# Second attention of a two-layer network: a query projection is given a PSUM bank of the other pair

## The chip, the cores and the metric

The kernel runs on one core of a Trainium2 chip. The metric is the device time of one execution in microseconds (us), the median of several; less is better.

## The reference

The reference takes 32 sequences of 128 tokens with 128 features and applies two layers, each of an attention and a feed-forward part with conditioning, all in fp32. The change lies in the attention of the second layer. That attention has 16 heads of 8 features, a causal mask and a layer norm:

```python
Q = jax.nn.relu(x @ Wq + bq)
K = jax.nn.relu(x @ Wk + bk)
V = jax.nn.relu(x @ Wv + bv)
...
scores = jnp.einsum('bqhd,bkhd->bhqk', Qh, Kh) / np.sqrt(dh)
...
attn = jax.nn.softmax(scores, axis=-1)
...
out = jnp.einsum('bhqk,bkhd->bqhd', attn, Vh).reshape(B, T, U)
out = out + x
...
return gamma * normalized + beta
```

Keys and queries whose token sums to zero are masked. The result is then multiplied by a per-sequence matrix (a base matrix plus a product of rank 8) before the last feed-forward part.

## The kernel before

The kernel is one program in which each engine has its own list of instructions, written out by hand, and the engines meet by counting semaphores. The second attention runs from about 645 to 856 us. It works in 32 blocks, one for each sequence; block q has four units of four heads (units 4q to 4q+3). Eight chunks of four sequences share one projection each of queries and keys.

Block q computes, spread over the engines:

- TensorE (`pe_attend2`): the scores of sequence q (`pe_S5`, L2113, 16 small matmuls into banks PB0 to PB3), the transposes of two units of the block before (`pe_T5`, units 4q-4 and 4q-3, L2141), in some blocks transposes of tokens or of the norm's output (L2249, L2343), the values of sequence q+1 (`pe_v5`, L2207), the product of weights and values of sequence q-2 (`pe_PV5`, L2158), in some blocks a projection (query L1623, key L1635, token sum L1632) or a product beside it (factors L2282 and L2288, select L2356, add L2367 and L2370), the transposes of units 4q-2 and 4q-1, and last the transposes of the attention's output of sequence q-2 (`pe_oT`, L2171).
- VectorE (`dve_attend2`): the norm of sequence q-3 (`dve_norm5`, L2180 to L2187), mask and maximum of the four units of block q (`dve_max5`, L2122, 16 instructions), with the layer norm's gamma step between the second and the third unit in every fourth block (`dve_gamma5`, L2349), then the bias of the values of sequence q+1 (`dve_v5`, L2212), statistics (L2199, L2201), and the steps beside (token-sum mask of the keys L1647, masks L2259 to L2263, factors L2300 and others).
- ScalarE (`act_attend2`): exponentials (L2134), the copies of transposed units out of PSUM (`act_pt5`, L2147), the copy of the attention's output (`act_o5`, L2165), the relu of a query or key projection (L1629, L1641), right behind that copy, and the norm's scaling (L2336).
- GpSimd (`pool_attend2`): subtraction of the maximum (L2129), relu and mask of the values (`pool_v5`, L2220 and L2221), a residual add (L2194) and the norm's root (L2325 to L2330).

The PSUM banks PB4 to PB7 are two pairs. A plan (`plan5`) walks through the program in TensorE's order and gives each result the next bank of its pair; `passes5` also records which semaphore says that the bank has been read out. Before a result is written, TensorE waits until the result two places earlier in the same pair has been read:

```python
def passes5(key, first, sem, value):
    through5[key] = first, len(drained5[first])
    drained5[first].append((sem, value))
...
def pe_drained5(key):
    first, n = through5[key]
    if n >= 2:
        pe.wait_ge(*drained5[first][n - 2])
```

The pair of PB4 and PB5 holds transposed units, the product with the values, queries and keys. The pair of PB6 and PB7 holds values, turned outputs, tokens, gamma, select, add, factors and the token sum. There are seven query projections in the plan: chunk 1 in block 1, chunk 2 in block 4, and chunks 3 to 7 in blocks 8, 12, 16, 20 and 24. The first chunk's was done before the attention began. The factors of the per-sequence matrices come in blocks 2, 3 and 4.

VectorE's bias of the values of sequence q+1 writes one of two buffers, so it waits (`dve.wait_ge(s_vy, 2 * (q - 2) + 1)`) until GpSimd has read the values two sequences earlier. For sequence 2, in block 1, that is GpSimd's first values step, which needs the masks of chunk 0.

Of the kernel before, what the change touches and what calls it, by code (L numbers as in the profile page):

```python
# [58 lines left out]
def build(nc, xT_d, w_d, out_d):  # L59
# [4 lines left out]
    with ctx:  # L64
# [3 lines left out]
        def signal(name):  # L68
            return ctx.enter_context(nc.semaphore(name))
# [897 lines left out]
        s_qp, s_qt, s_qz, s_be = signal("q_mm"), signal("q_relu"), signal("spread_zero"), signal("beta")  # L967
# [1051 lines left out]
# [3 lines that stand above are left out]

        def plan_aside(what, c):
            if what == "query":
                passes5(("q", c), 4, s_qt, c + 1)
            if what == "key":
                passes5(("k", c), 4, s_kt, c + 1)
            if what == "keysum":
                passes5(("ks", c), 6, s_kx, c + 1)
            if what == "tokens":  # L2030
                passes5(("x", c), 6, s_xc, c + 1)
            if what == "b1":
                passes5("b1", 6, s_b1, 3)
            if what == "factors":
                passes5(("f", c), 6, s_facd, c + 1)
            if what == "gamma":
                passes5(("T", c), 6, s_fd, 3 * c + 1)
            if what == "select":
                passes5(("A", c), 6, s_fd, 3 * c + 2)
            if what == "add":  # L2040
                passes5(("B", c), 6, s_fd, 3 * c + 3)

        def plan_asides(q, kinds):
            for s in range(4 * q, 4 * q + 4):
                for what, c in aside(s):
                    if what in kinds:
                        plan_aside(what, c)
# [9 lines left out]
        def plan5():  # L2057
            passes5(("x", 0), 6, s_xc, 1)
            passes5(("v", 0), 6, s_vt, 1)
            for q in range(NB5):  # L2060
                plan_T5(4 * q - 4)
                plan_T5(4 * q - 3)
                plan_asides(q, TURNED)
                if q + 1 < NB5:
                    passes5(("v", q + 1), 6, s_vt, q + 2)
                if q >= 2:
                    passes5(("o", q - 2), 4, s_o5, q - 1)
                plan_asides(q, PROJECTED)
                plan_asides(q, MULTIPLIED)
                plan_T5(4 * q - 2)  # L2070
                plan_T5(4 * q - 1)
                if q >= 2:
                    passes5(("oT", q - 2), 6, s_nd, 4 * (q - 2) + 4)
            for u in range(U - 4, U):
                plan_T5(u)
                if u == U - 4:
                    passes5(("o", NB5 - 2), 4, s_o5, NB5 - 1)
                if u == U - 3:
                    plan_aside("gamma", 6)
            passes5(("oT", NB5 - 2), 6, s_nd, 4 * (NB5 - 2) + 4)  # L2080
            plan_aside("select", 6)
            passes5(("o", NB5 - 1), 4, s_o5, NB5)
            passes5(("oT", NB5 - 1), 6, s_nd, 4 * (NB5 - 1) + 4)
            plan_aside("add", 6)
            for what in FINISH.values():
                plan_aside(what, 7)
# [1158 lines left out]
```

## Time and profile before

| | us |
|---|---|
| median of 3 runs | 955.68 |
| lowest and highest | 955.13, 956.82 |
| the profiled execution, its own time | 954.23 |
| its span on the core | 952.9 |
| mean granted TensorE clock, share of full | 0.996 |

| engine | busy us | share of the span |
|---|---|---|
| PE (TensorE matmul) | 918.1 | 96% |
| PEld (TensorE weight load) | 734.3 | 77% |
| DVE (VectorE) | 789.0 | 83% |
| ACT (ScalarE) | 796.1 | 84% |
| POOL (GpSimd) | 548.5 | 58% |

All times in the rows are us from the start of the span. A matmul row gives its start and the time until its modelled end; the next matmul may start before that end, since matmuls are pipelined. So the pace of TensorE is read from the starts. A bracket at a row's end says how long the engine sat idle before it and which instruction ended that. SPq is the queue of DMA issues.

### The profile page before, as it was taken

What the parts mean: (1) busy time and instruction counts of PE and PEld (TensorE: products, weight loads), DVE (VectorE), ACT (ScalarE), POOL (GpSimd) and SP (SyncE); (2) the same over time, 40 slices, a digit from 0 to 9 for tenths busy, and PEclk for the clock granted to TensorE, in tenths of its full rate; (3) what the DMA queues carried; (4) which work ended last, traced back from release to release, by engine and by line L of the source; (5) the groups of instructions that cost most, each with busy time, mean ns of one, the idle gap of its engine ahead of it and who ended that gap; (6) DMA issues with size and microseconds to landing.
All of it is one profiled execution on the core that took longest, in us unless ns stands there. A gap on an engine that the chain in (4) does not pass through costs nothing.

```text
span 952.9 us, 25813 instructions
## 1 busy us (share of the span) xinstructions
PE 918.1 (96%) x8641; PEld 734.3 (77%) x8641; DVE 789.0 (83%) x3563; ACT 796.1 (84%) x2162; POOL 548.5 (58%) x670
## 2 busy tenths in 40 slices
PE   8999999999999999999999999999989999999887
PEld 8899989899998989973225888877877777775566
DVE  6766998989898989989997766758889889896985
ACT  7998989898988888867875989987788888886886
POOL 4444636465564646451796148757789898891041
PEclk9999999999999999999999999999999999999899
DMA  9100000000000000000236899911000000000002
GB/s 372 69 2 2 2 2 2 2 2 2 2 1 2 2 2 2 2 2 0 89 115 195 283 304 306 318 63 33 24 20 18 24 17 21 24 3 1 2 1 89
DMA packets 36226, 57.70 MB, mean 61 GB/s; under 512 B 3456, under 2 KB 27264, under 8 KB 35712
## 3 DMA queue, kind: packets, MB, share of 16 engines
q1 hardware_dynamic: 36096, 56.07, 17.6%
q8 instruction: 69, 1.13, 0.5%
q14 instruction: 61, 0.50, 0.2%
HBM read 40.85 MB, written 11.01 MB: 54 GB/s over the span
## 4 chain that ended last, share of the span: by engine, by line
PE 64%; DVE 17%; ACT 9%; POOL 4%; issue 4%; DMA 0%; SPq 0%; ACTq 0%; DVEq 0%; POOLq 0%
PE PB L270 6%; PE PB L271 5%; PE PB L272 5%; PE PB L437 5%; PE PB L2141 5%; PE PB L390 4%; PE PB L459 3%; PE PB L2113 3%; PE PB L2158 3%; DVE W L400 2%; ACT W L409 2%; PE PB L1423 2%; PE PB L1424 2%; PE PB L1425 2%; DVE HFXT L607 1%
## 5 line engine op out<-in xcount | busy, mean ns | idle before, releaser
L409 ACT ACTIVATE W<-W,small 128x128 f32<-128x128 f32 x384 | 149.0, 392 | 11.4 <-DVE small L400 10.6
L421 POOL TENSOR_TENSOR W<-W,small 128x512 f32<-128x512 f32 x96 | 100.7, 1054 | 100.2 <-DVE small L415 100.2
L270 PE MATMUL PB<-RR_s 128*128 128x256 f32 (+1 forms) x468 | 153.2, 327 | 3.4 <-DVE RR_s L471 1.4
L271 PE MATMUL PB<-RR_s 128*128 128x256 f32 (+1 forms) x468 | 140.0, 299 | 0.0
L272 PE MATMUL PB<-RR_s 128*128 128x256 f32 (+1 forms) x468 | 139.8, 299 | 0.0
L2129 POOL TENSOR_TENSOR AR_s<-AR_s,small 128x512 f32<-128x512 f32 x128 | 129.9, 1045 | 15.4 <-DVE small L2122 15.4
L2122 DVE CUSTOM_DVE_ANT_0 AR_s<-PB,W 128x128 f32<-128x128 f32 x512 | 111.2, 286 | 2.1 <-PE PB L2113 0.3
L270 PEld LDWEIGHTS PB<-RR_s 128*128 128x128 f32 x468 | 88.8, 190 | 19.0 <-issue 7.8
L1399 DVE TENSOR_TENSOR RR_s<-AR_s,RR_s 128x512 fp32r<-128x512 f32 (+1 forms) x96 | 65.7, 689 | 43.0 <-ACT RR_s L1392 39.1
L400 DVE CUSTOM_DVE_ANT_0 W<-PB,W 128x128 f32<-128x128 f32 x384 | 85.9, 282 | 13.5 <-PE PB L390 12.8
L349 DVE COPY AR_s<-PB 128x512 f32<-128x512 f32 x128 | 84.9, 684 | 13.6 <-PE PB L272 13.0
L271 PEld LDWEIGHTS PB<-RR_s 128*128 128x128 f32 x468 | 89.0, 190 | 3.5 <-issue 0.7
L272 PEld LDWEIGHTS PB<-RR_s 128*128 128x128 f32 x468 | 88.6, 189 | 3.0
L2134 ACT ACTIVATE AR_s<-AR_s 128x512 f32<-128x512 f32 x128 | 79.7, 625 | 10.6 <-POOL AR_s L2129 10.1
L2147 ACT ACTIVATE AR_s<-PB 128x512 f32<-128x512 f32 x128 | 72.5, 593 | 17.8 <-PE PB L2141 17.5
L443 ACT ACTIVATE HFXT<-PB 128x512 f32<-128x512 f32 x123 | 73.4, 597 | 16.7 <-PE PB L437 14.6
L2141 PEld LDWEIGHTS PB<-W,AR_s 128*128 128x128 f32 x512 | 56.5, 141 | 26.7 <-issue 12.2
L2141 PE MATMUL PB<-W,AR_s 128*128 128x128 f32 x512 | 70.9, 278 | 5.2 <-ACT AR_s L2165 2.7
L409 ACT ACTIVATION_READ_ACCUMULATOR W<-W,small 128x1 f32 x384 | 73.2, 191 | 0.0
L1457 POOL TENSOR_TENSOR HFXT<-HFXT,AR_s 128x128 f32 x68 | 41.3, 636 | 54.5 <-DVE AR_s L1447 54.4
L390 PE MATMUL PB<-AR_s 64*128 64x128 f32 x1024 | 65.8, 278 | 0.0
L1392 ACT ACTIVATE RR_s<-AR_s 128x512 fp32r<-128x512 f32 (+1 forms) x96 | 57.3, 597 | 8.5
(461 smaller groups left out, 2635.0 us busy)
## 6 DMA issues: line engine op xcount, KB each, us to landing
RR_s<-W1D SPq DMA_DIRECT2D x13, 512.0 KB, 4.3
RR_s<-W2D SPq DMA_DIRECT2D x13, 512.0 KB, 4.5
W<-in_w SPq DMA_DIRECT2D x1, 5895.5 KB, 24.9
RR_s<-XD SPq DMA_DIRECT2D x46, 128.0 KB, 3.0
XD<-RR_s SPq DMA_DIRECT2D x18, 256.0 KB, 3.6
HQ<-W1D SPq DMA_DIRECT2D x6, 512.0 KB, 4.3
HQ<-W2D SPq DMA_DIRECT2D x6, 512.0 KB, 4.8
HQ<-XD SPq DMA_DIRECT2D x22, 128.0 KB, 3.2
```

The costliest lines, as they stand in the source:

```text
L270: nc.tensor.matmul(out, lh, rh, start=True, stop=False)
L271: nc.tensor.matmul(out, ll, rh, start=False, stop=False)
L272: return nc.tensor.matmul(out, lh, rl, start=False, stop=True)
L349: nc.vector.tensor_copy(QK[v % 2][pr], bank("k", n)[:, :]).then_inc(s_qk, 1)
L390: mm = nc.tensor.matmul(score(u, h), qk[r, b * 128:b * 128 + 128], qk[r, 256 + b * 128:256 + b * 128 + 128], start=True, stop=True)
L400: nc.vector.tensor_tensor_reduce(SS[r][:, hl], score(u, h), w("mask"), -0.125, 3.0e38, ALU.add, ALU.min, mx[r][:, h:h + 1]).then_inc(s_max, 1)
L409: e = nc.scalar.activation(SS[r][:, hl], SS[r][:, hl], ACTF.Exp, bias=mx[r][:, h:h + 1], scale=-1.0, accum_out=rc[r][:, h:h + 1])
L421: nc.gpsimd.tensor_tensor(s3, s3, over(rc[r], 2, [128, 4, 128]), ALU.mult).then_inc(s_nrm, 1)
L2122: nc.vector.tensor_tensor_reduce(SS5[r][:, hl], score5(u, h), w("mask"), isq8, -3.0e38, ALU.add, ALU.max, mx5[r][:, h:h + 1]).then_inc(s_m ...
L2129: nc.gpsimd.tensor_tensor(s3, s3, over(mx5[r], 2, [128, 4, 128]), ALU.subtract).then_inc(s_sub, 1)
L2134: nc.scalar.activation(SS5[r], SS5[r], ACTF.Exp).then_inc(s_ex5, 1)
L2141: mm = nc.tensor.transpose(bank5(("p", u))[:, hl], SS5[u % 6][:, hl], ident)
```

## The change

The query projection of a chunk is planned in the pair PB6 and PB7 where it was planned in PB4 and PB5. One number of the plan changes:

```diff
         def plan_aside(what, c):
             if what == "query":
-                passes5(("q", c), 4, s_qt, c + 1)
+                passes5(("q", c), 6, s_qt, c + 1)
             if what == "key":
                 passes5(("k", c), 4, s_kt, c + 1)
             if what == "keysum":
```

No instruction is added, removed or moved on any engine. What changes is the bank of each result behind a query, and, since each result waits for the one two places earlier in its pair, what TensorE waits for around each of the seven queries. In the rows below `v5_bias` is the semaphore of VectorE's bias of the values (L2212), `pt5` that of ScalarE's copy of a transposed unit (L2147), `o5` that of the copy of the output (L2165), `q_relu` and `k_relu` those of the relus (L1629, L1641), `norm5` that of VectorE's norm (L2180 to L2187), and `finish_dve` here that of the gamma step (L2349).

The first place is TensorE in block 1, from the values of sequence 2 to the scores of block 2. Before:

```order
L2207 MATMUL PB7<-W,HFXT 128x128 [waits v5_bias]
L1623 MATMUL PB4<-HFXT,W 128x512 [waits pt5]
L1635 MATMUL PB5<-HFXT,W 128x512 [waits pt5]
L1632 MATMUL PB6<-HFXT,small 128x512 [waits v5_bias]
L2141 MATMUL PB4<-W,AR_s5 128x128 [waits exp5,q_relu]
L2141 MATMUL PB4<-W,AR_s5 128x128 x3
L2141 MATMUL PB5<-W,AR_s5 128x128 [waits exp5,k_relu]
L2141 MATMUL PB5<-W,AR_s5 128x128 x3
L2113 MATMUL PB0<-KR0,QS0 128x128 [waits max5]
```

With the change:

```order
L2207 MATMUL PB7<-W,HFXT 128x128 [waits v5_bias]
L1623 MATMUL PB6<-HFXT,W 128x512 [waits v5_bias]
L1635 MATMUL PB4<-HFXT,W 128x512 [waits pt5]
L1632 MATMUL PB7<-HFXT,small 128x512 [waits v5_bias]
L2141 MATMUL PB5<-W,AR_s5 128x128 [waits exp5,pt5]
L2141 MATMUL PB5<-W,AR_s5 128x128 x3
L2141 MATMUL PB4<-W,AR_s5 128x128 [waits exp5,k_relu]
L2141 MATMUL PB4<-W,AR_s5 128x128 x3
L2113 MATMUL PB0<-KR0,QS0 128x128 [waits max5]
```

The query (L1623) now waits for a value's bias and the transposes behind it no longer wait for the query's relu. The token sum (L1632) takes the next bank of the same pair: the name of its semaphore is as before, but the result two places earlier was the value of sequence 1 and is now that of sequence 2.

The second place is TensorE in block 8, from the gamma transposes to the scores of block 9; blocks 12, 16, 20 and 24 read the same. Before:

```order
L2343 MATMUL PB6<-W,AR_s5 128x128 [waits ln_applied,v5_bias]
L2343 MATMUL PB6<-W,AR_s5 128x128 x3
L2207 MATMUL PB7<-W,HFXT 128x128 [waits norm5]
L2158 MATMUL PB4<-AR_s5 32x128 [waits pt5,vy]
L2158 MATMUL PB4<-AR_s5 32x128 x15
L1623 MATMUL PB5<-HFXT,W 128x512 [waits pt5]
L2141 MATMUL PB4<-W,AR_s5 128x128 [waits exp5,o5]
L2141 MATMUL PB4<-W,AR_s5 128x128 x3
L2141 MATMUL PB5<-W,AR_s5 128x128 [waits exp5,q_relu]
L2141 MATMUL PB5<-W,AR_s5 128x128 x3
L2171 MATMUL PB6<-W,AR_s5 128x128 [waits finish_dve]
L2171 MATMUL PB6<-W,AR_s5 128x128 x3
```

With the change:

```order
L2343 MATMUL PB6<-W,AR_s5 128x128 [waits ln_applied,v5_bias]
L2343 MATMUL PB6<-W,AR_s5 128x128 x3
L2207 MATMUL PB7<-W,HFXT 128x128 [waits norm5]
L2158 MATMUL PB4<-AR_s5 32x128 [waits pt5,vy]
L2158 MATMUL PB4<-AR_s5 32x128 x15
L1623 MATMUL PB6<-HFXT,W 128x512 [waits finish_dve]
L2141 MATMUL PB5<-W,AR_s5 128x128 [waits exp5,pt5]
L2141 MATMUL PB5<-W,AR_s5 128x128 x3
L2141 MATMUL PB4<-W,AR_s5 128x128 [waits exp5,o5]
L2141 MATMUL PB4<-W,AR_s5 128x128 x3
L2171 MATMUL PB7<-W,AR_s5 128x128 [waits v5_bias]
L2171 MATMUL PB7<-W,AR_s5 128x128 x3
```

The query waits for the gamma step where it waited for a copy. The second group of transposes behind it waits for the copy of the output where it waited for the query's relu, the first group for a copy of a unit. The turned output (L2171) waits for the bias of the values of sequence 9, written in the same block, where it waited for the gamma step.

The third place is TensorE in block 4, as the difference of the two; L2288 are the factors, L2171 the turned output of sequence 2.

```order
-L1623 MATMUL PB<-HFXT,W 128x512 [waits pt5]
-L2288 MATMUL PB<-W,HFXT 128x128 [waits norm5]
+L1623 MATMUL PB<-HFXT,W 128x512 [waits norm5]
+L2288 MATMUL PB<-W,HFXT 128x128 [waits v5_bias]
 L2288 MATMUL PB<-W,HFXT 128x128 x7
+L2141 MATMUL PB<-W,AR_s 128x128 [waits exp5,pt5]
+L2141 MATMUL PB<-W,AR_s 128x128 x3
 L2141 MATMUL PB<-W,AR_s 128x128 [waits exp5,o5]
 L2141 MATMUL PB<-W,AR_s 128x128 x3
-L2141 MATMUL PB<-W,AR_s 128x128 [waits exp5,q_relu]
```

The factors now wait for the bias of the values of sequence 5, where they waited for the norm of sequence 1.

## Rows read from the trace of the kernel before

**Rows 1.** The chain of waits, block 16: start, us, what.

```profile
757.05 0.70 ACT AR_s L1629
...
757.79 0.66 PE PB L2141 x4
```

**Rows 2.** Waits from 640 to 850 us: in total, times, longest.

```profile
PE PB L2141 <- ACT AR_s L2165: 2.7, 3, 1.9
...
PE PB L2141 <- ACT AR_s L1629: 2.0, 5, 0.4
```

**Rows 3.** Timeline of TensorE, block 16 from the query on.

```profile
755.83 1.13 PE L1623 MATMUL PB<-HFXT,W 128*128 128x512 f32 x2
756.79 0.60 PE L2141 MATMUL PB<-W,AR_s 128*128 128x128 f32 x4
757.79 0.66 PE L2141 MATMUL PB<-W,AR_s 128*128 128x128 f32 x4 [0.40 <-ACT AR_s L1629]
758.29 0.60 PE L2171 MATMUL PB<-W,AR_s 128*128 128x128 f32 x4
```

**Rows 4.** Timeline of ScalarE and VectorE, block 16.

```profile
756.03 0.60 ACT L2165 ACTIVATE AR_s<-PB 128x512 f32<-128x512 f32 x1
...
759.16 0.60 ACT L2147 ACTIVATE AR_s<-PB 128x512 f32<-128x512 f32 x1
...
755.08 0.75 DVE L2349 SCALAR_TENSOR_TENSOR XF<-PB,W,XF 128x512 f32<-128x512 f32 x1
...
757.42 0.28 DVE L2212 TENSOR_TENSOR AR_s<-PB,W 128x128 f32<-128x128 f32 x1
...
758.92 0.24 DVE L2180 TENSOR_SCALAR small<-PB,small 128x16 f32<-128x16 f32 x1 [0.80 <-PE PB L2171]
```

**Rows 5.** Timeline of TensorE, block 1 to the scores of block 2.

```profile
654.14 1.13 PE L1623 MATMUL PB<-HFXT,W 128*128 128x512 f32 x2 [0.64 <-ACT AR_s L2147]
...
655.97 1.02 PE L1632 MATMUL PB<-HFXT,small 128*128 128x512 f32 x2
656.82 1.04 PE L2141 MATMUL PB<-W,AR_s 128*128 128x128 f32 x8
657.79 1.17 PE L2113 MATMUL PB<-KR,QS 32*128 32x128 f32 x32
```

**Rows 6.** Timeline of ScalarE, GpSimd and VectorE, block 1.

```profile
653.52 1.06 ACT L2147 ACTIVATE AR_s<-PB 128x512 f32<-128x512 f32 x2
...
657.36 0.73 POOL L2220 TENSOR_SCALAR AR_s<-AR_s,small 128x128 f32<-128x128 f32 x1 [0.35 <-DVE small L2263]
...
658.19 0.29 DVE L2212 TENSOR_TENSOR AR_s<-PB,W 128x128 f32<-128x128 f32 x1 [0.95 <-POOL AR_s L2220]
```

**Rows 7.** Timeline of TensorE and VectorE, block 4.

```profile
676.19 1.95 PE L2288 MATMUL PB<-W,HFXT 128*128 128x128 f32 x16
...
676.41 0.29 DVE L2212 TENSOR_TENSOR AR_s<-PB,W 128x128 f32<-128x128 f32 x1
```

**Rows 8.** The chain of waits, blocks 6 and 7, and TensorE's timeline there.

```profile
688.51 2.71 POOL AR_s L2129 x3
...
696.82 0.61 ACT AR_s L2134
...
697.96 0.65 PE L2141 MATMUL PB<-W,AR_s 128*128 128x128 f32 x4 [1.94 <-ACT AR_s L2165]
```

**Rows 9.** Windows: us, busy PE, PEld, DVE, ACT, POOL, granted clock, DMA, GB/s.

```profile
885.00:890.00 5.00, 3.80 (x22) 2.67 (x24) 4.83 (x35) 4.20 (x10) 0.00 (x0) 0.76 0.00 0
890.00:895.00 5.00, 5.00 (x28) 4.20 (x29) 3.94 (x24) 2.50 (x7) 0.00 (x0) 0.55 0.00 0
...
695.00:700.00 5.00, 3.06 (x60) 2.42 (x52) 3.76 (x30) 4.74 (x11) 4.98 (x7) 1.00 0.01 3
```

**Rows 10.** Timeline of TensorE around the fall of the clock.

```profile
885.01 0.66 PE L2625 MATMUL PB<-W,HFXT 128*128 128x128 f32 x4 [1.48 <-DVE AR_s L2581]
...
888.88 1.11 PE L2656 MATMUL PB<-W,AR_s 128*128 128x128 f32 x4 [1.19 <-DVE AR_s L2581]
```

## The prediction

> **What bounds the kernel now.** The chain of waits comes first, since the change touches nothing but what TensorE waits for. From 640 to 850 us that chain runs through TensorE nearly all the time, and in block 16 it leaves TensorE for one instruction, the query's relu on ScalarE, and comes back with the transposes behind it [rows 1]. The list of waits says how often: TensorE stood still for this relu in five blocks, 2.0 us in total, and for the copy of the output three times, 2.7 us in total and 1.9 of it at once [rows 2]; hardly any other wait of its own matmuls is in that list. The timeline of block 16 then gives the pace, read from the starts: query 755.83, four transposes 756.79, four more 757.79, turned output 758.29 [rows 3]. VectorE meanwhile waited 0.80 us for the turned output [rows 4], so TensorE is late there and not early. The timelines of blocks 1 and 4 [rows 5 to 7] are read for what the new waits meet, and blocks 6 and 7 [rows 8] and the granted clock [rows 9, 10] for what a delay does further on.
>
> **Blocks 8, 12, 16, 20 and 24: the relu's wait goes.** Transposes follow each other without a wait at 0.50 us or less per four (757.79 to 758.29 [rows 3]). The first four start at 756.79 in any case. The second four need the copy of the output, which ends at 756.63 (756.03 + 0.60 [rows 4]), and the end of the first four, so they can start at about 757.24 and not 757.79. The turned output would follow at 757.70. It now waits for the bias of the values instead, which ends at 757.70 (757.42 + 0.28 [rows 4]); with the few hundredths of a us that a semaphore takes (relu end 757.74, transposes 757.79 [rows 1, 3, 4]) it starts at 757.75 or so. The query's own new wait, for the gamma step, ends at 755.83 (755.08 + 0.75 [rows 4]), the very start of the query [rows 3]; it costs about 0.05 us. So the turned output comes 0.54 us earlier. What is late next: the scores follow it, and the block's second copy of transposed units ends at 759.76 (759.16 + 0.60 [rows 4]), for which the second unit of the next block waits. ScalarE does not get faster, since its relu still begins when the query's matmuls end. Moved up by 0.54, that unit would start within 0.1 us of this copy's end, so I take off 0.1: 0.44 us per block, 2.2 us in five. The bounds are 2.7 (all of 0.54) and 1.5 (0.3 each, if the tight waits for gamma and bias each cost 0.1 more). The cover for VectorE is its 0.80 us wait for the turned output [rows 4]; 0.26 of it is left.
>
> **Block 1: the token sum gets a late wait.** Of the two banks of its pair it takes the one of the values of sequence 2. Their bias on VectorE waits for GpSimd's first values step, which waits for the masks: it ends at 658.48 (658.19 + 0.29 [rows 6]). The token sum starts at 655.97 today [rows 5]. Nothing upstream of that bias hangs on the query, so it stays where it is, and the token sum starts at 658.53. Behind it in TensorE's order are the transposes of units 2 and 3 and the scores of block 2, and everybody waits for the scores. From 655.97 to 657.79 it is 1.82 us [rows 5]; a matmul whose weights are not loaded ahead adds 0.1 (755.83 to 756.79 is 0.96 [rows 3] where 655.97 to 656.82 is 0.85 [rows 5]). The scores start at 660.45, not 657.79: 2.7 us, bounds 2.5 and 2.8. The query and the key may start earlier (the key waits for the first of two copies, which is over by 654.1 [rows 6]), which only makes the pause longer, up to 3.5 us: nothing else stands between them and the token sum. VectorE's mask of the keys waits for the token sum, but is done before the scores. The DMAs that spread the keys wait for that mask, and are read three blocks later, so they are hidden; nothing is queued behind them that is due sooner.
>
> **Block 4: the same in small.** The second factors start at 676.19 and now wait for the bias of the values of sequence 5, over at 676.70 (676.41 + 0.29 [rows 7]). With the semaphore that is 0.56, with the weight load up to 0.66: I take 0.6, bounds 0.5 and 0.7. The relu there is hidden behind the 1.95 us of factors [rows 7], so nothing is won.
>
> **Is a delay given back?** By the list of waits TensorE has hardly a gap from block 2 on [rows 2], so a late start of the scores is passed on. The one place with slack is block 7, where TensorE waits 1.94 us for ScalarE [rows 8]. But the chain there is GpSimd's subtraction at 688.51, which waits for VectorE's maxima, which wait for the scores of block 6; then its root, ScalarE's scaling and exponential at 696.82 [rows 8]. It moves with TensorE. I take 0 given back; the far bound is all of 1.94.
>
> **The clock.** TensorE's granted clock was at the full 2.4 GHz through the whole attention. It fell to 1.2 GHz once in the body of the kernel, after two pauses of 1.48 and 1.19 us within four us [rows 10], and the two windows there make the low stretch 2 x (0.24 + 0.45) x 5 = 6.9 us [rows 9]. The single pause of 1.94 us in block 7 left it at 1.00 [rows 8, 9]. The new pause in block 1, 2.6 to 3.5 us, is longer than any in this trace, so I expect a fall there. At half the clock the work in the low stretch takes twice its time, so half the low stretch that falls on work is lost: 3.4 us if all of 6.9 does. In the row at hand 1.2 us of it was the second pause, leaving 5.7 and a loss of 2.8. Behind one long pause the fall may come in the pause itself, and the work behind it is dense, which should bring the clock back sooner. Between 0 and 3.4 I take 2.1. The Trainium skill, "TensorE: Matmul & The Clock Gate", Part 1, speaks against the change here: the array's clock is halved after a stretch of idleness and comes back only under sustained work. By that rule the sum has this term, without it it does not; the fall in the row at 887 us agrees with it, and no run here yet shows which pause is long enough.
>
> **The sum.** +2.7 + 0.6 - 2.2 + 2.1 = +3.2 us. The profiled execution took 954.23, 1.33 outside its span of 952.9, so it would become 957.4. It lies 1.45 below the median of 955.68; on the median the forecast is 958.9. With the bounds it runs from +1.6 (2.5 + 0.5 - 2.7 + 1.3) to +5.4 (2.8 + 0.7 - 1.5 + 3.4).
>
> **Rivals.**
> 1. The clock holds. For it: no pause in this attention moved the clock. Against it: the row at 885 to 890. Then +1.1: 956.8, no measurable difference. It decides from a fall that costs under 0.8 us.
> 2. The pause is given back, the other side of my forecast: one mechanism, block 7. If GpSimd's chain there keeps its own time, TensorE's 1.94 us shrink to nothing and the total is +1.1 - 1.9 = -0.8 with the clock up: 954.9. It decides once more than 1.1 us is given back. Against it: the chain starts from the scores.
> 3. The relu's wait is replaced. In blocks 8 to 24 the bias of the values ends where the turned output would start, and the gamma step where the query does. If VectorE is 0.5 us later there than I read, the gain is 0 and the total 2.7 + 0.6 + 2.1 = +5.4: 961.1.
> 4. The change does not do what it says, because the relu was not what the transposes waited for but something that ends with it. The rows name the relu, and ScalarE's copy ends 1.1 us earlier, so this falls together with case 3.
>
> **How the numbers follow.** A measurement of this kernel can tell about 0.2% from no change, 1.9 us: faster is under 953.8, slower over 957.6. Forecast 0.63, rival 1 0.24, rival 2 0.06, rivals 3 and 4 0.07. Of the forecast nearly all is slower, of rival 1 one part in eight, of 3 all: 0.66. Faster would take rival 2 with a gain at its upper bound, or a wait that I misread: 0.04. The rest, 0.30, is the same. The range of 8 in 10 takes in rival 1 down to 955.6 and the forecast and most of rival 3 up to 960.6.
>
> **What would show it.** Block 1: the token sum starts near 658.5 with a bracket that names L2212, the scores of block 2 near 660.4. Block 4: the factors start about 0.5 us after their old place in the block. Blocks 8 to 24: no bracket for L1629, the turned output 1.9 us after the query where it was 2.5. Clock: a window under 1.00 between 655 and 667. It is wrong if the scores of block 2 start before 659.5, if L1629 still ends a wait of TensorE, or if block 7's wait is much shorter than 1.94.

## The result, and the profile after

| | before | changed |
|---|---|---|
| median of 20 runs, us | 955.93 | 960.23 |
| lowest and highest, us | 954.31, 959.08 | 956.26, 963.59 |
| the profiled execution, us | 954.23 | 959.01 |
| its span, us | 952.9 | 957.7 |
| mean granted clock in it | 0.996 | 0.992 |

The ratio of the changed kernel to the one before is 1.0035, with a 95% interval of 1.0027 to 1.0044: 3.3 us more (2.6 to 4.2). The means of the 20 runs differ by 3.5 us, the medians by 4.3. The forecast was 3.2 us more, 958.9; the median of 960.23 lies in the predicted range of 955.6 to 960.6, near its upper end. The kernel is slower by more than a measurement of it leaves open. The two profiled executions differ by 4.8 us; 0.5 of that is there before the second attention begins and has nothing to do with the change.

The list of waits of the changed kernel, from 640 to 850 us, has no entry for the query's relu (L1629) any more, and three new ones. The columns are as in [rows 2].

```profile
PE PB L1632 <- DVE AR_s L2212: 3.3, 1, 3.3
PE PB L2141 <- ACT AR_s L2165: 2.7, 3, 1.9
...
PE PB L2158 <- ACT AR_s L2147: 0.9, 5, 0.2
...
PE PB L2288 <- DVE AR_s L2212: 0.4, 1, 0.4
```

The biggest new wait is the token sum's in block 1. TensorE's timeline there, to be laid beside [rows 5]:

```profile
653.61 0.39 PE L2207 MATMUL PB<-W,HFXT 128*128 128x128 f32 x2
653.83 1.02 PE L1623 MATMUL PB<-HFXT,W 128*128 128x512 f32 x2
654.69 1.07 PE L1635 MATMUL PB<-HFXT,W 128*128 128x512 f32 x2
659.02 1.51 PE L1632 MATMUL PB<-HFXT,small 128*128 128x512 f32 x2 [3.26 <-DVE AR_s L2212]
660.32 1.91 PE L2141 MATMUL PB<-W,AR_s 128*128 128x128 f32 x8
662.16 1.57 PE L2113 MATMUL PB<-KR,QS 32*128 32x128 f32 x32
```

And VectorE's, for [rows 6]:

```profile
658.67 0.29 DVE L2212 TENSOR_TENSOR AR_s<-PB,W 128x128 f32<-128x128 f32 x1 [0.95 <-POOL AR_s L2220]
```

The query and the key start earlier than before, as they may, and then TensorE stands for 3.26 us until the bias of the values of sequence 2 is done (658.67 + 0.29 = 658.96). Counted from the values of sequence 2 (L2207), which takes the 0.5 us from before the attention out of the comparison, the token sum comes at +5.41 where it came at +2.85, and the scores of block 2 at +8.55 (662.16 - 653.61) where they came at +4.67. The eight transposes behind the pause take 1.84 us from start to start (660.32 to 662.16) and not 0.97 (656.82 to 657.79 [rows 5]). That is the clock. The windows, with the columns of [rows 9], for both places where it was below 1.00 in this attention:

```profile
655.00:658.00 3.00, 0.76 (x2) 0.00 (x0) 2.65 (x13) 2.26 (x5) 2.66 (x4) 1.00 0.09 22
658.00:661.00 3.00, 1.98 (x6) 1.14 (x7) 0.72 (x2) 0.00 (x0) 2.39 (x6) 0.77 0.26 66
661.00:664.00 3.00, 3.00 (x41) 2.55 (x40) 0.34 (x2) 2.12 (x4) 0.00 (x0) 0.66 0.25 61
664.00:667.00 3.00, 3.00 (x51) 2.68 (x49) 3.00 (x29) 2.56 (x5) 2.06 (x3) 1.00 0.10 27
702.00:705.00 3.00, 1.61 (x12) 1.28 (x16) 1.50 (x12) 3.00 (x7) 3.00 (x4) 0.83 0.01 3
705.00:708.00 3.00, 3.00 (x41) 2.78 (x42) 2.01 (x13) 1.10 (x3) 1.40 (x4) 0.60 0.00 0
```

The clock went to 1.2 GHz (0.50) behind the new pause for 2 x (0.23 + 0.34) x 3 = 3.4 us, and again in block 7, behind the old pause of 1.94 us that had left it alone in the trace before [rows 8, 9].

Block 4 reads as forecast too; the factors wait 0.40 us:

```profile
680.00 1.12 PE L1623 MATMUL PB<-HFXT,W 128*128 128x512 f32 x2
681.53 2.05 PE L2288 MATMUL PB<-W,HFXT 128*128 128x128 f32 x16 [0.40 <-DVE AR_s L2212]
```

And block 16, TensorE, for [rows 3], with the first half of block 17:

```profile
761.97 1.12 PE L1623 MATMUL PB<-HFXT,W 128*128 128x512 f32 x2
762.93 1.04 PE L2141 MATMUL PB<-W,AR_s 128*128 128x128 f32 x8
763.86 0.66 PE L2171 MATMUL PB<-W,AR_s 128*128 128x128 f32 x4
764.44 1.17 PE L2113 MATMUL PB<-KR,QS 32*128 32x128 f32 x32
765.55 1.09 PE L2141 MATMUL PB<-W,AR_s 128*128 128x128 f32 x8
767.04 1.08 PE L2158 MATMUL PB<-AR_s 128*32 128x128 f32 x32 [0.18 <-ACT AR_s L2147]
```

The eight transposes run without a gap, and the turned output starts 1.89 us after the query, not 2.46. In the next block the product with the values (L2158) waits 0.18 us for a copy of a transposed unit, in five blocks.

### The profile page after: what moved, and what is told of

Its sections match the earlier page's. It is cut to its first block, busy times and chain, and to the rows that moved or that the text cites. A ratio compares the mean times of both kernels' runs of the same rounds, so it can differ in the third digit from the quotient of the medians.

```text
span 957.7 us, 25813 instructions
## 1 busy us (share of the span) xinstructions
PE 920.5 (96%) x8641; PEld 735.1 (77%) x8641; DVE 789.2 (82%) x3563; ACT 794.9 (83%) x2162; POOL 548.1 (57%) x670
## 4 chain that ended last, share of the span: by engine, by line
PE 65%; DVE 18%; ACT 9%; POOL 4%; issue 4%; DMA 0%; SPq 0%; DVEq 0%; ACTq 0%; POOLq 0%
PE PB L270 7%; PE PB L271 6%; PE PB L272 6%; PE PB L437 5%; PE PB L2141 5%; PE PB L390 4%; PE PB L459 3%; PE PB L2158 3%; PE PB L2113 3%; DVE W L400 2%; ACT W L409 2%; PE PB L1423 2%; PE PB L1425 2%; PE PB L1424 2%; DVE HFXT L607 1%
## 5 line engine op out<-in xcount | busy, mean ns | idle before, releaser
L2147 ACT ACTIVATE AR_s<-PB 128x512 f32<-128x512 f32 x128 | 72.5, 593 | 23.3 <-PE PB L2141 23.1
```

## The experiments

All were timed beside the kernel before on the same chip, three or four kernels to a session. The ratios carry their 95% intervals; the time over the kernel before is the ratio applied to 956.5 us, the median of the kernel before in these sessions. The sessions are the first four rows, the next four and the last three; each kernel has 5 to 12 executions in them.

| kernel | median us | ratio to before | us over before |
|---|---|---|---|
| chunk 1 only | 961.22 | 1.0052 (1.0033 to 1.007) | +5.0 |
| chunks 3 to 7 | 954.11 | 0.9982 (0.9969 to 0.9996) | -1.7 |
| chunks 2 to 7 | 955.55 | 0.9989 (0.9974 to 1.0003) | -1.1 |
| all, pause of block 1 filled | 957.21 | 1.0006 (0.9993 to 1.0019) | +0.6 |
| chunks 3 to 7, pause of block 7 filled | 953.67 | 0.9969 (0.9956 to 0.9981) | -3.0 |
| chunk 1 only, pause of block 1 filled | 958.89 | 1.0025 (1.0012 to 1.0039) | +2.4 |
| all, again | 960.64 | 1.0044 (1.0027 to 1.0062) | +4.2 |
| all, third buffer | 958.23 | 1.0024 (1.0007 to 1.0041) | +2.3 |
| none, pause of block 7 filled | 955.45 | 0.9988 (0.9979 to 0.9997) | -1.1 |
| chunks 3 to 7, again | 954.47 | 0.9976 (0.9965 to 0.9987) | -2.3 |
| chunks 3 to 7, block 7 filled, again | 953.72 | 0.9961 (0.9948 to 0.9975) | -3.7 |

Kernels that have the same instructions up to a place agree there to a few hundredths of a us, so each term below is read from the traces, and the ratios only have to agree. All starts are counted from the values of sequence 2 (L2207) in block 1.

| kernel | token sum | scores, block 2 | turned output, block 2 | block 4 | block 7 | block 8 |
|---|---|---|---|---|---|---|
| before | 2.85 | 4.67 | 11.18 | 25.72 | 45.34 | 52.12 |
| all | 5.41 | 8.55 | 15.47 | 30.68 | 50.27 | 57.98 |
| chunk 1 only | 5.42 | 7.35 | 13.86 | 28.39 | 48.00 | 56.33 |
| chunks 3 to 7 | 2.85 | 4.68 | 11.19 | 25.73 | 45.34 | 53.05 |
| chunks 2 to 7 | 2.85 | 4.68 | 11.19 | 26.40 | 45.98 | 53.69 |
| all, block 1 filled | 5.41 | 7.34 | 13.86 | 29.06 | 48.66 | 56.36 |
| chunks 3 to 7, block 7 filled | 2.85 | 4.67 | 11.18 | 25.72 | 45.32 | 51.58 |

The row of chunks 3 to 7 is the first of its two traces; its second agrees to 0.02 us, and so do the two with block 7 filled. The token sum is L1632 in block 1, the scores are L2113; the last four columns are the turned outputs (L2171) of blocks 2, 4, 7 and 8.

**One chunk at a time: chunk 1.**

```diff
-                passes5(("q", c), 6, s_qt, c + 1)
+                passes5(("q", c), 6 if c == 1 else 4, s_qt, c + 1)
```

> Only the query of chunk 1 (block 1) takes a bank of PB6 and PB7. My theory: the token sum of block 1 waits about 3.3 us for L2212, and the scores of block 2 come 2.7 us later than before when the clock holds and about 4.3 later when it falls behind the pause; nothing else of the second attention changes. So 2.7 to 4.4 us over the kernel before, and five waits for L1629 remain. Rival (the pause is made good in block 7): under 1 us over it, with block 7's wait much shorter than 1.94.

In its profiled execution the clock did not fall behind the pause of block 1, though the pause was as long, to the hundredth:

```profile
655.40 1.02 PE L1623 MATMUL PB<-HFXT,W 128*128 128x512 f32 x2
656.26 1.07 PE L1635 MATMUL PB<-HFXT,W 128*128 128x512 f32 x2
660.59 1.12 PE L1632 MATMUL PB<-HFXT,small 128*128 128x512 f32 x2 [3.26 <-DVE AR_s L2212]
661.55 1.04 PE L2141 MATMUL PB<-W,AR_s 128*128 128x128 f32 x8
662.52 1.17 PE L2113 MATMUL PB<-KR,QS 32*128 32x128 f32 x32
```

So this trace gives the wait alone: scores at +7.35, against +4.67, is 2.68 us. The changed kernel's own trace has the same wait and the fall, and is at +15.47 in block 2's turned output where this one is at +13.86: the fall costs 1.61 us. Nothing is given back afterwards: 2.68 at block 2, 2.67 at block 4 (28.39 - 25.72), 2.66 at block 7. The time over the kernel before, 5.0 us, is above the 2.7 to 4.4 that I gave, though its interval (3.2 to 6.7) reaches into it. What the trace shows beyond the wait is a fall of the clock behind the pause of block 7, in which this kernel still has the old order: block 8 comes 8.33 us after block 7 (56.33 - 48.00) and not 6.78, 1.55 us for the fall. Why the median is so high is not shown.

**Chunks 3 to 7.**

```diff
-                passes5(("q", c), 6, s_qt, c + 1)
+                passes5(("q", c), 6 if c >= 3 else 4, s_qt, c + 1)
```

> The queries of chunks 3 to 7 (blocks 8, 12, 16, 20, 24) take a bank of PB6 and PB7, those of chunks 1 and 2 stay. My theory: no wait for L1629 is left and nothing is added, each block ends about 0.4 us earlier: 2.0 us under the kernel before (1.5 to 2.7). Rival (the relu's wait is replaced by the bias of the values): within 0.5 us of the kernel before, with waits for L2212 of about 0.4 us each.

> Chunks 3 to 7 moved, again, beside the others on one chip. By my theory 2.0 us under the kernel before (1.5 to 2.7).

1.7 and 2.3 us under the kernel before, about the theory's 2.0. The whole gain of the change lies in these five chunks, and the rival (a new wait for L2212 of about 0.4 us in each) falls: no such wait is in the list. Of the first of the two, the windows behind block 7's pause:

```profile
698.00:701.00 3.00, 1.06 (x8) 0.82 (x9) 2.48 (x21) 3.00 (x8) 3.00 (x4) 1.00 0.02 5
701.00:704.00 3.00, 3.00 (x40) 2.57 (x39) 1.25 (x5) 1.99 (x4) 2.47 (x5) 0.57 0.00 0
704.00:707.00 3.00, 3.00 (x47) 2.68 (x46) 2.79 (x22) 1.79 (x3) 2.05 (x2) 0.86 0.02 5
```

The clock fell there as well, in a kernel that differs from the one before by nothing up to that point. Block 8 ends 7.71 us after block 7 (53.05 - 45.34) with the fall and 6.26 (51.58 - 45.32) without it in the kernel with the pause filled: 1.45 us for this fall. It is not of the change, since the instructions up to there are those of the kernel before. Nor is it rare: of the ten traces in this document with this pause unfilled, eight show a fall behind it, and only those of the kernel before and of the one with the third buffer do not.

**Chunks 2 to 7.**

```diff
-                passes5(("q", c), 6, s_qt, c + 1)
+                passes5(("q", c), 6 if c >= 2 else 4, s_qt, c + 1)
```

> As the run before, and the query of chunk 2 (block 4) moved too. My theory: the factors of block 4 wait for L2212 and cost 0.6 to 0.7 us, so 1.4 us under the kernel before. Rival (the factors' wait is covered by something behind it): as the run without chunk 2, about 2.0 us under.

1.1 us under the kernel before by the ratio, 0.67 us later in block 4 by the trace (26.40 against 25.73), and still 0.64 later in block 7. The rival, that something covers this wait, falls by the trace; the intervals of this kernel and of the one without chunk 2 are too wide to part the two by time.

**The pause of block 1, filled.** Three matmuls whose result nobody reads go into a bank of the scores, after the maxima of block 1 have read it. Here the edit on the changed kernel; the other run has it on the kernel with chunk 1 alone.

```diff
                 steps_of(projected, q)
+                if q == 1:
+                    pe.wait_ge(s_mx5, 32)
+                    for _ in range(3):
+                        nc.tensor.matmul(PB[0][:, :], w("aq"), cs(HF, 1), start=True, stop=True)
                 steps_of(multiplied, q)
```

> The changed kernel with three added matmuls of 128x512 in the pause of block 1, into a bank of the scores that nobody reads, so that TensorE is busy for 2.6 us of it. The result of the program is the same. My theory (what the pause costs beyond its length is the clock, which falls behind it): the clock stays at 1.00 in blocks 1 and 2, and the program is 1.5 to 2 us faster than the changed kernel, about 1.5 to 2.5 us over the kernel before. Rival (beyond its length the pause costs nothing, or costs it by the late weight loads): same time as the changed kernel, about 4 us over the kernel before.

> Only the query of chunk 1 moved, with three added matmuls in the pause of block 1. The result of the program is the same. My theory: the wait alone, without the clock, is left: 2.7 us over the kernel before, 1.5 to 2 us under the same kernel without the filling. Rival (the pause costs more by itself than 2.7, for instance by late copies on ScalarE): 3.5 to 4.5 us over the kernel before.

```profile
658.12 2.84 PE L2938 MATMUL PB<-HFXT,W 128*128 128x512 f32 x6 [0.20 <-DVE small L2122]
661.17 1.12 PE L1632 MATMUL PB<-HFXT,small 128*128 128x512 f32 x2 [0.22 <-DVE AR_s L2212]
662.14 1.04 PE L2141 MATMUL PB<-W,AR_s 128*128 128x128 f32 x8
663.10 1.17 PE L2113 MATMUL PB<-KR,QS 32*128 32x128 f32 x32
```

Its window over the token sum and the transposes:

```profile
661.00:664.00 3.00, 2.83 (x41) 2.13 (x42) 0.81 (x2) 1.23 (x3) 1.54 (x4) 1.00 0.13 35
```

The token sum comes at the same +5.41 as in the changed kernel, since the wait is untouched, but the clock is at 1.00 and the scores come at +7.34 and not +8.55. More work for TensorE made the program faster. By the ratios the changed kernel goes from 1.0035 and 1.0044 to 1.0006, some 3 us, more than the 1.5 to 2 expected; the intervals (1.0027 to 1.0044 and 0.9993 to 1.0019) do not overlap. The traces account for 1.61 us of it (15.47 - 13.86 at the turned output of block 2); where the rest comes from is open. The unfilled pause of block 7 still has a fall behind it in both filled kernels' traces (7.70 us from block 7 to block 8 in this one). With chunk 1 alone the filling leaves +2.4 us (1.2 to 3.7), about the 2.7 of the bare wait. The rival, that the pause costs its surplus by late copies or weight loads, falls: the same pause without a fall, in the trace of chunk 1 alone, costs 2.68 us and no more.

**The changed kernel again.**

> The changed kernel itself, beside the others on the same chip. By my theory 3 to 4.5 us over the kernel before, and where its trace shows no fall of the clock behind block 1 the scores of block 2 come 2.7 us late, where it shows one about 4.3.

4.2 us over the kernel before. Its trace has a fall of 3.4 us behind block 1 and one behind block 7, and the scores of block 2 come at +8.59, 3.9 late; by the turned output of block 2, where the fall is over, it is the 4.3 that I gave.

**A third buffer.** The changed kernel, with the biased values of sequence 2 in a buffer of their own.

```diff
-            dve.wait_ge(s_vy, 2 * (q - 2) + 1)
-            nc.vector.tensor_tensor(VT[q % 2], bank5(("v", q))[:, 0:128], w("bv"), ALU.add).then_inc(s_vt, 1)
+            if q != 2:
+                dve.wait_ge(s_vy, 2 * (q - 2) + 1)
+            nc.vector.tensor_tensor(VT[2 if q == 2 else q % 2], bank5(("v", q))[:, 0:128], w("bv"), ALU.add).then_inc(s_vt, 1)
```

> The changed kernel, with a third buffer for the biased values of sequence 2, so that L2212 of that sequence does not wait for GpSimd's first values step. My theory: the bias ends about 0.9 us earlier (at the end of the masks plus 0.3), the token sum starts 0.9 earlier, and the clock falls in fewer executions: 0.9 to 1.6 us under the changed kernel. Rival (something else holds the token sum, for instance the key's projection or its relu): same time as the changed kernel, and the token sum starts where it did.

```profile
659.15 1.12 PE L1632 MATMUL PB<-HFXT,small 128*128 128x512 f32 x2 [2.17 <-DVE AR_s L2214]
```

GpSimd's read of these values is changed to the same buffer, which is taken from an unused stretch; neither is printed above. L2214 is the L2212 of the other kernels. The values of sequence 2 start at 654.82 there, so the token sum comes at +4.33: 1.08 us earlier than in the changed kernel (0.9 expected), and the pause shrinks from 3.26 to 2.17. The program is 2.3 us over the kernel before and not 3.3 or 4.2; that is 2.0 us under the changed kernel of its session by the ratios (0.9 to 1.6 expected), though the two intervals overlap (1.0007 to 1.0041 and 1.0027 to 1.0062). By the trace the chain is as read: token sum behind VectorE's bias, behind GpSimd's values step, behind the masks. The clock did not fall in its attention in the profiled execution, but that was the fastest of its twelve (955.9 to 964.0 us), so whether a shorter pause makes falls rarer is not shown.

**The pause of block 7, filled.** Two matmuls go into the bank that the turned output takes next. The edit was made on the kernel with chunks 3 to 7 (timed twice) and on the kernel before.

```diff
                 if q:
                     pe_T5(4 * q - 2)
+                if q == 7:
+                    pe_drained5(("oT", 5))
+                    for _ in range(2):
+                        nc.tensor.matmul(bank5(("oT", 5))[:, :], w("aq"), cs(HF, 1), start=True, stop=True)
+                if q:
                     pe_T5(4 * q - 1)
```

> The kernel with chunks 3 to 7 moved (blocks 8 to 24) and two added matmuls of 128x512 in TensorE's pause of 1.94 us in block 7, into the free bank that the turned output takes next. The result of the program is the same. My theory: in some executions the clock falls behind this pause and costs about 1.5 us; with the pause filled it does not, so the slow ones among the runs go and the median is 0.5 to 1.5 us under that of the kernel without the filling, about 3 us under the kernel before. Rival (the spread of the runs comes from elsewhere): the median and the spread as without the filling.

> The kernel before, with the two added matmuls in TensorE's pause of block 7 and no query moved. The result of the program is the same. My theory: the filling saves about 1.5 us in those executions in which the clock would fall behind the pause, and nothing in the others: 0.3 to 1.0 us under the kernel before in the median, and no fall between 690 and 710 us in its trace. Rival (the filling itself shortens something): 1.5 us or more under it.

> Chunks 3 to 7 moved and the pause of block 7 filled, again, beside the others. By my theory the sum of the two runs beside it: 2.3 to 3.2 us under the kernel before. Rival (the first measurement of this kernel was chance): no more under it than chunks 3 to 7 moved alone.

```profile
696.87 0.66 PE L2141 MATMUL PB<-W,AR_s 128*128 128x128 f32 x4
697.36 1.88 PE L2941 MATMUL PB<-HFXT,W 128*128 128x512 f32 x4
699.45 0.66 PE L2141 MATMUL PB<-W,AR_s 128*128 128x128 f32 x4 [0.21 <-ACT AR_s L2165]
```

The turned output of block 7 comes at +45.32, as before (+45.34): the matmuls fit into the pause and lengthen nothing. On the kernel before they save 1.1 us in the median (0.3 to 2.0; expected 0.3 to 1.0). By time alone the rival, that the filling itself shortens something, is not excluded; the trace speaks against it, since without a fall in either the turned output of block 8 comes at +52.10 with the filling and at +52.12 without. On the kernel with chunks 3 to 7 the two sessions give 3.0 and 3.7 us under the kernel before with them, against 1.7 and 2.3 without: the sign is the same twice, while the intervals overlap. None of the three traces has a fall of the clock between 690 and 710 us, where eight of the ten unfilled ones have. The spread agrees: without the filling, the kernel with chunks 3 to 7 ran from 953.03 to 957.34 us and again from 953.53 to 955.90, with it from 952.27 to 955.10 and from 952.83 to 954.71. This kernel, 953.7 us in both sessions, beats both the kernel before and the changed one.

## Why the prediction was right

**Block 1: 2.7 us forecast, 2.68 measured.** The wait, its releaser, its start after the end of VectorE's bias and the extra 0.1 us for weights that are not loaded ahead are all in the trace of chunk 1 alone. The brackets name the instruction that was forecast.

**The clock: 2.1 forecast, 1.61 measured for the fall behind block 1.** The fall came where it was forecast, in two of three traces, and the term was a little large. I had reckoned from a low stretch of 6.9 us [rows 9]; the one behind the pause is 3.4 us. It did not begin in the pause, as I had allowed for, but at about 659.6 (661.00 - 2 x 0.23 x 3), some 0.6 us after the token sum's start, so nearly all of it falls on work, and half of that is lost. I had also misread the old fall. The window in which it begins puts it at about 887.6. By then TensorE had stood still only for the first of the two pauses, 1.48 us; the second, of 1.19 us, ends at 888.88 [rows 10] and so had not begun:

```profile
887.50:887.75 0.25, 0.19 (x2) 0.00 (x0) 0.25 (x2) 0.00 (x0) 0.00 (x0) 0.78 0.00 0
```

So a pause shorter than the 1.94 us of block 7 already stood before a fall, and my reason for taking block 7 as safe and block 1 as not, the length of the pause, was weak. What I had not seen is that the fall is not certain for a given pause. The same pause of 3.26 us had a fall in two of three traces, and the pause of 1.94 us in block 7, which I had set down as harmless from one trace, had one in eight of ten traces. In the 20 runs of the changed kernel the twelve with a mean granted clock of 0.993 or less took 959.0 to 963.6 us, the eight with 0.994 or more 956.3 to 958.8, which takes in the 956.8 of rival 1, no fall. So forecast and rival 1 may both have happened, in different executions. The mean clock alone does not show it, since it does not say where a fall lies: the trace of chunk 1 alone has 0.996 with a fall behind block 7, and the trace before has 0.996 with none in the attention, because its fall at 887.6 lasted 6.8 us and the one there 3.4. The Trainium skill, "TensorE: Matmul & The Clock Gate", Part 1, calls the number of matmuls before the clock rises run-variable for the same kernel. No run here shows that count at a kernel's start; what varies here between executions is whether the clock falls.

**Block 4: 0.6 forecast, 0.67 measured.** Upper half of the bounds.

**Blocks 8 to 24: 0.44 each forecast, 0.41 to 0.43 measured.** At the turned output the gain is 0.52 us (6.78 from block 7 to block 8 before, 6.26 with block 7 filled), where I had 0.54. What takes 0.1 back is ScalarE, as forecast, but not where I put it: not the second unit's transposes wait for the block's last copy; the product with the values (L2158) waits for the first copy of the next block, five times. In block 16 the relu begins 1.22 us after the query in both kernels, and ScalarE's five instructions behind it kept their time after the query to 0.02 us. The copies that follow were 0.34 us late for want of transposes before; now they come 4.32 us after the query and not 4.78, a gain of 0.46 where TensorE had gained 0.57 from the query to the turned output:

```profile
765.77 0.64 ACT L2134 ACTIVATE AR_s<-AR_s 128x512 f32<-128x512 f32 x1
766.29 1.09 ACT L2147 ACTIVATE AR_s<-PB 128x512 f32<-128x512 f32 x2
```

**The sum.** For the profiled execution: 2.68 + 1.61 + 0.67 - 5 x 0.42 + 1.5 for the second fall = 4.4 us over the attention, where the trace shows 4.3 (4.82 at the turned outputs of the last blocks, less the 0.49 from before it). In the forecast the first four terms are 3.2 against 2.9 measured, and the second fall was not in it; in the other direction, the kernel before probably has such falls in some of its executions too, though its one trace shows none. That the 3.2 of the forecast stands beside a ratio of 3.3 us is therefore partly luck: the terms of the waits are right to 0.1 us each, the clock's share varies from execution to execution. The forecast's lower end of +1.6 took 1.3 us for the clock, for which it gives no source, though its text allows for 0.

**The rivals.** Rival 1, that the clock holds, is the case in one of three traces with the pause, where the wait costs its 2.68 us alone. Rival 2, that block 7 gives the pause back, falls: its wait is 1.92 in the changed kernel, and chunk 1 alone keeps 2.66 of 2.68 us up to there. Rival 3, that a wait for L2212 replaces the relu's, falls with the list of waits; the bias and the turned output do meet within a few hundredths, but the bias is not late. Rival 4 falls with the wait list, from which L1629 is gone.

## What to carry to other kernels

When results take turns in the banks of a pair and each waits for the one two places before, adding a member to a pair moves the waits of every neighbour, so list the partner of each one: here the member moved won 0.4 us in five places, and its neighbour, the token sum, lost more in one. An exception for the first chunks of a pipeline, where the late partner is set by start-up work, kept the gain and dropped the loss. Price a pause of TensorE at its length and at the chance of a slower clock behind it, from more than one trace, and if it can't be removed, try filling it with matmuls that nobody reads.

## What the runs showed of the hardware

The fall of the granted clock to 1.2 GHz behind a pause differs between executions of one program: 3.26 us of standing still brought it in two traces and not in a third, 1.9 us brought it in eight of ten traces, the changed kernel's among them, and not in those of the kernel before and of the third buffer. Behind the attention, in the kernel before, a fall began at 887.6 after 1.48 us of standing still. Each fall in the attention lasted 3.4 us, and three of them, read above, cost 1.45, 1.55 and 1.61 us of TensorE's time. Idle matmuls in the pause, 2.8 us of them in one and 1.9 us in the other, left no such fall behind that pause in any of the five traces.
